# A convolution, attention and expert kernel: projection moved ahead of the next contraction, side work in other slots

## The chip, the cores and the metric

The kernel runs on one core of one Trainium2 chip. The metric is the device time of one execution in microseconds. The core has five engines that run side by side and wait for each other through semaphores: TensorE (PE), VectorE (DVE), ScalarE (ACT), GpSimd (POOL) and SyncE (SP), whose queue issues most DMAs. PE writes only to PSUM, which has eight banks of 128 x 512 fp32 numbers.

## The reference

Four images of 32 x 32 positions and 128 channels go through two layers, each added to its input.

1. A group norm, then a deformable convolution: eight groups of 32 channels, nine samples a position. Offsets, a scale and weights come from projections of the normalised image; each sample is a bilinear mix of four values; the eight groups' sums are projected by `out_w` and added to the image.
2. A layer norm and attention through 32 slices for each of eight heads, added; then a layer norm and a mixture of eight experts (128 to 512 to 128, exact GELU), of which each position uses its best two, added.

```python
x = x + conv(_gn(x), ...)
t = _to_tokens(x)
t = t + attn(_ln_t(t), ...)
t = t + ffn(_ln_t(t), ...)
```

## The kernel before

**Main loop.** The convolution is done as matrix products instead of gathers. There are 32 groups (`ig`, four images of eight), each of four batches (`beta`) of two half steps (`pair`), 256 half steps (`k`) in all. In a half step `distances` (L746) makes the distances of samples to grid rows and columns in banks 4 and 5; ACT turns the one into ramps (L1047, L1057), DVE (L1355, `take_y`) and POOL (L670, `ysb`) the other; `products` (L759) multiplies them, 64 small matmuls, into banks 0 and 1 (pair 0) or 2 and 3 (pair 1); DVE copies them out (L1365, `take`, into `asb`). The first three stages run three half steps ahead. After eight half steps `contract` (L774) contracts `asb` with the values into banks 0 to 3, ACT copies the result to `osp` (L1064, `spread_out`), `project` (L782) multiplies it by `out_w` into banks 2 and 3, and DVE adds it to the image (L1374, `conv_add`).

**Side work.** Each engine runs its own program in order. Between the half steps it calls `side` with a slot number. A group has nine slots, one for each half step and one more between the last products and the contraction; an image has 72. While image 0 is contracted, the slots hold the preparation of images 1 to 3 (`prepare`, 23 slots an image). While image b is contracted they hold image b-1's attention (23 pieces, `attend`, slots 2 to 30), the sorting of its tokens by expert (POOL, `sort_rows` L638, slots 29 to 36), the turning of the sorted rows (40 to 45) and its 23 expert tiles (46 to 69), and image b-2's picking and adding of rows (`pick_rows` L648, `add_rows` L1593, slots 1 to 17). A tile is `hidden` (L934, PE), `gelu` (L1132, ACT), `finish` (L947, PE) and `copy_rows` (L1583, DVE). All of this uses banks 6 and 7 alone, so each step of it waits until the step before has left them.

**Tail.** Behind the last contraction the attention and the experts of image 3 follow, with all eight banks and twelve buffers for expert weights instead of four; POOL picks image 2's rows first.

**Order.** It is written out by hand: the tables of slots at the top say on which engine which step is called when. At a group's start PE does the distances, the first side slot and the first products; then the distances, `project` of the group before, the second side slot; the second products wait for `conv_add`, since they write banks 2 and 3. DVE does `take_y`, the side slot, `take` in each half step, with `conv_add` ahead of the second.

## Time and profile before

| | us |
|---|---|
| median of three runs | 1490.27 (1489.19 to 1490.53) |
| the profiled execution | 1483.1, span 1481.2 |
| busy: PE, DVE, ACT, POOL | 1076.1, 907.2, 729.4, 695.7 |
| DMA | 80 GB/s in the mean |

An engine's busy time says how long it worked, not whether anyone waited for it. The span has four parts: what lies ahead of the first contraction (to 89.6 us), image 0's contraction with the preparation of the others (to 354.1), images 1 to 3 with the side work (to 1288.4), and the tail. Waits are put down to the instruction that released them. PE's busy time includes the modelled ends of pipelined matmuls.

### The profile page before, as it was taken

The page shows a single profiled execution, that of the slowest core. Times are in us where ns is not written, and L with a number is a line of the kernel's source. Part 1 is how long each engine was busy: PE and PEld are TensorE (multiplying, and loading weights), DVE is VectorE, ACT ScalarE, POOL GpSimd, SP SyncE. Part 2 cuts the span into 40 slices and gives each one's busy share as a digit, 9 for nine tenths or more (in the row PEclk, how much of TensorE's full clock was granted, in tenths as well). Part 3 has the DMA queues.
Part 4 walks back from the last instruction along what each step waited for, and adds up shares of the span by engine and source line. Part 5 has one row for each costly group of instructions (what it writes and reads, how often), then busy time and mean ns, then how long its engine had stood idle before and what let it go on. Part 6 is the DMA issues. An engine that isn't in the chain of part 4 may idle for free.

```text
span 1481.2 us, 62984 instructions
## 1 busy us (share of the span) xinstructions
PE 1076.1 (73%) x27983; PEld 879.2 (59%) x28236; DVE 907.2 (61%) x1619; ACT 729.4 (49%) x1403; POOL 695.7 (47%) x675
## 2 busy tenths in 40 slices
PE   3476766866886678986876789968866799765390
PEld 2365655645565568875565678856655688635290
DVE  7578775786756664458876564467666744454311
ACT  1454653545563456664643666655534566331060
POOL 6355544544432754457434744474427644510304
PEclk9598987999997899998987999999978999976595
DMA  6503222022000324631012325521103345200861
GB/s 143 143 27 92 67 47 96 27 54 99 24 26 15 105 76 125 177 101 35 26 40 84 90 64 160 148 68 31 35 22 99 83 139 151 73 9 1 254 185 55
DMA packets 166288, 121.96 MB, mean 82 GB/s; under 512 B 45641, under 2 KB 146050, under 8 KB 165506
## 3 DMA queue, kind: packets, MB, share of 16 engines
q1 hardware_dynamic: 161922, 109.53, 26.1%
q0 software_dynamic: 4096, 8.40, 1.8%
q8 instruction: 222, 3.64, 1.0%
q14 instruction: 48, 0.39, 0.1%
HBM read 89.38 MB, written 28.51 MB: 80 GB/s over the span
## 4 chain that ended last, share of the span: by engine, by line
PE 53%; DVE 25%; issue 11%; POOL 5%; ACT 3%; DMA 1%; another core or an unknown queue 1%; DVEq 0%; POOLq 0%; ACTq 0%
PE ps L774 13%; PE ps L759 12%; PE ps L934 6%; PE ps L947 6%; DVE asb L1365 5%; PE ps L746 4%; DVE yr L1355 4%; PE ps L782 3%; POOL ysb L670 2%; POOL picked L648 2%; DVE region L1577 1%; POOL sorted_rows L638 1%; DVE x_tok L1374 1%; PE ps L857 1%; PE ps L711 1%
## 5 line engine op out<-in xcount | busy, mean ns | idle before, releaser
L670 POOL TENSOR_TENSOR ysb<-yr,rw 128x512 f32<-128x512 f32 x512 | 547.1, 1093 | 567.3 <-DVE yr L1355 499.6
L1365 DVE COPY asb<-ps 128x1024 f32<-128x1024 f32 x256 | 312.0, 1219 | 126.1 <-PE ps L759 124.7
L759 PE MATMUL ps<-xsb,ysb 64*64 64x64 f32 x16384 | 324.2, 231 | 60.3 <-DVE x_tok L1374 38.3
L759 PEld LDWEIGHTS ps<-xsb,ysb 64*64 64x64 f32 x16384 | 287.0, 144 | 134.4 <-issue 111.4
L1057 ACT ACTIVATE xsb<-xr,pick 128x512 f32<-128x512 f32 x512 | 361.9, 764 | 4.4
L1355 DVE TENSOR_SCALAR yr<-ps 128x512 f32<-128x512 f32 x256 | 174.3, 681 | 218.1 <-PE ps L746 210.9
L774 PE MATMUL ps<-asb,vd 32*32 32x256 f32 x8192 | 204.2, 443 | 86.3 <-DVE asb L1365 68.3
L774 PEld LDWEIGHTS ps<-asb,vd 32*32 32x32 f32 x8192 | 146.1, 111 | 137.3 <-issue 109.8
L1047 ACT ACTIVATE xr<-ps 128x512 f32<-128x512 f32 x256 | 151.7, 593 | 137.4 <-remote 137.1
L746 PE MATMUL ps<-spread_b,lp 128*128 128x512 bf16 x259 | 105.5, 409 | 122.1 <-DVE yr L1355 51.1
L1064 ACT ACTIVATE osp<-ps 128x256 f32<-128x256 f32 x128 | 39.8, 405 | 277.3 <-PE ps L774 277.3
L1132 ACT ACTIVATE region<-ps,b_col 128x128 f32<-128x128 f32 x368 | 105.1, 370 | 88.5 <-PE ps L934 88.5
L638 POOL DMA_INDIRECT sorted_rows<-region,row_no x64 | 62.8, 982 | 116.2 <-DVE row_no L1545 100.5
L648 POOL DMA_INDIRECT picked<-expert_rows,row_no x64 | 61.7, 964 | 90.5 <-DMA expert_rows<-region 73.7
L746 PEld LDWEIGHTS ps<-spread_b,lp 128*128 128x128 bf16 x512 | 33.4, 98 | 117.9 <-DVE yr L1355 47.9
L934 PEld LDWEIGHTS ps<-region,ring 128*128 128x128 f32 x616 | 80.7, 195 | 9.5 <-issue 1.4
L934 PE MATMUL ps<-region,ring 128*128 128x128 f32 x616 | 83.6, 280 | 1.3 <-issue 1.3
L947 PE MATMUL ps<-ring,region 128*128 128x128 f32 x616 | 82.0, 276 | 0.0
L947 PEld LDWEIGHTS ps<-ring,region 128*128 128x128 f32 x616 | 75.7, 193 | 0.4
L1583 DVE COPY region<-ps 128x128 f32<-128x128 f32 x92 | 26.8, 291 | 74.8 <-PE ps L947 74.8
L782 PEld LDWEIGHTS ps<-outw,osp 128*128 128x128 f32 x512 | 62.1, 192 | 6.3 <-ACT osp L1064 1.8
L782 PE MATMUL ps<-outw,osp 128*128 128x128 f32 x512 | 62.4, 275 | 1.3 <-ACT osp L1064 1.3
(235 smaller groups left out, 1075.9 us busy)
## 6 DMA issues: line engine op xcount, KB each, us to landing
ring<-in_L_ffn_W SPq DMA_DIRECT2D x154, 256.0 KB, 3.1
vd<-group_values SPq DMA_DIRECT2D x128, 128.0 KB, 2.7
asb<-in_L_ffn_W SPq DMA_DIRECT2D x30, 256.0 KB, 4.3
lp<-position_parts SPq DMA_DIRECT2D x96, 64.0 KB, 2.4
position_parts<-region SPq DMA_DIRECT2D x3, 1536.0 KB, 6.0
group_values<-region SPq DMA_DIRECT2D x32, 128.0 KB, 3.5
weight_rows<-region SPq DMA_DIRECT2D x4, 1024.0 KB, 6.1
rw<-weight_rows SPq DMA_DIRECT2D x32, 128.0 KB
```

The source lines that it names most:

```text
L670: pl.tensor_tensor(ysb[:, n % 2, pair * CHUNK:(pair + 1) * CHUNK, u, :], yr[:, k % 3, :, :], rw[:, ig % 2, u, first:first + CHUNK].rearran ...
L746: pe.matmul(ps[:, bank, :], lp[:, ig % 2, beta, d, :], spread_b[:, half * CHUNK:(half + 1) * CHUNK, :].rearrange("p s q -> p (s q)"), star ...
L759: last = pe.matmul(o[:, :, NV * q:NV * q + NV], ysb[rows, n % 2, col, :, :].rearrange("p u y -> p (u y)"), xsb[rows, n % 2, col, :, :], st ...
L774: last = pe.matmul(ps[32 * jc:32 * jc + 32, j, 0:256], vd[rows, ig % 2, x, :], asb[rows, x, :, :, :].rearrange("p i n m -> p (i n m)"), st ...
L782: last = pe.matmul(pcol(2, t), osp[:, t, :], outw[:, ig % G, :], start=True, stop=True)
L934: last = pe.matmul(ps[:, hidden_bank(b, i), j * P:(j + 1) * P], ring_part(r, 0)[:, j * P:(j + 1) * P], xsT[:, i, :], start=True, stop=True)
L947: last = pe.matmul(ps[:, expert_bank(b, i), 0:C], hT[:, i % 2, j, :], ring_part(r, 1)[:, j * P:(j + 1) * P], start=(j == 0), stop=(j == HJ ...
L1047: act.activation(xr[:, half * CHUNK:(half + 1) * CHUNK, :].rearrange("p s q -> p (s q)"), ps[:, X_BANK, :], ACT.Relu, bias=1.0, scale=-1.0 ...
L1057: act.activation(xsb[:, n % 2, sets, :, v], xr[:, sets, :], ACT.Relu, bias=pick[:, v:v + 1], scale=-1.0).then_inc(s.x_ready, 1)
L1132: last = act.activation(hT[:, i % 2, j, :], ps[:, hidden_bank(b, i), j * P:(j + 1) * P], ACT.Gelu, bias=b1_col[:, i, j:j + 1])
L1355: dve.tensor_scalar(yr[:, k % 3, :, :].rearrange("p s q -> p (s q)"), ps[:, Y_BANK, :], 0.0, 1.0, ALU.max, ALU.min).then_inc(s.y_taken, 1)
L1365: dve.tensor_copy(asb[:, :, :, 2 * beta + pair, :].rearrange("p x i m -> p i x m"), ps[:, 2 * pair:2 * pair + 2, :].rearrange("p i (x m) - ...
```

## The change

- `project` of group g is called at the end of group g+1, in front of `contract`, and writes banks 6 and 7 (the last group: 2 and 3 as before). In an image's first group it is called in the second half step, for the image before. The second products wait for ACT's copies out of banks 2 and 3 instead of for `conv_add`. DVE calls `conv_add` behind the group's last `take`.
- Since banks 6 and 7 are the side work's too, PE waits ahead of `project` until the latest side step has been evacuated (`wait_for_banks`), and ahead of the next side slot until `conv_added`.
- A group has eight slots, an image 64. The tables are new. A slot serves image b-1 and, with its number raised by 64, image b-2 (`works`). The last expert tiles (slots 64, 66, 67, 68), the picking (72 to 79) and the adding (80 to 87) fall into the next image's first 24 slots. The tail goes through the same slots, now with image 2's last tiles, picking and adding in it.
- DVE's longer steps are cut into several with slots of their own: the reciprocal (two halves of 256 columns), statistics and normalisation, the choice of experts (`find_top`, `find_gates`), the columns (three parts), and in the preparation `find_places`, `split_places` and `edge_weights`.
- The attention's and the preparation's weights are turned in slot 5 instead of 69. `row_diff`, `parts_late`, `stage` and `rows_in` have other places in the shared region, and the waits that guard them have moved with them.
- The sort starts in slot 30, with the rows' numbers made in slot 29 (before: 29 and 27).

```diff
-ATTENTION = 23
-
-
-GROUP_SLOTS = 2 * BATCHES + 1
+
+
+GROUP_SLOTS = 2 * BATCHES
 SLOTS = G * GROUP_SLOTS
 
-PREP_SLOTS = 23
-PE_PREP = ((0, 0), (3, 2), (4, 3)) + tuple((7 + t, 4 + t) for t in range(NT)) + ((20, 13), (21, 14))
-ACT_PREP = ((0, 0), (4, 3), (15, 12), (20, 13), (21, 14))
-DVE_PREP = (((1, 1), (3, 2), (5, 3), (6, 15)) + tuple((7 + t, 4 + t) for t in range(NT))
-            + ((15, 16), (16, 12), (17, 19), (18, 17), (19, 18)))
-SP_PREP = ((14, 11), (19, 12), (21, 14))
-TURN_SLOT, BIAS_SLOT = PREP_SLOTS * (B - 1), PREP_SLOTS * (B - 1) + 2
-
-ATTENTION_SLOTS = (2, 3, 5, 6, 7, 8, 10, 11, 12, 13, 14, 15, 17, 18, 19, 20, 21, 22, 23, 24, 27, 29, 30)
-WEIGHT_SLOT = 28
-SORT_SLOT, SORT_SLOTS = 29, 8
-ROW_SLOT = 37
-TURN_ROWS_SLOT = 40
-TILE_SLOT = 46
-PICK_SLOT, PICK_SLOTS = 1, 8
-ADD_SLOT = 10
+PREP_SLOTS = 20
+COLUMN_SLOTS = (6, 7, 8, 9, 10, 11, 12, 12)
+PE_PREP = ((0, 0), (2, 2), (3, 3)) + tuple((COLUMN_SLOTS[t], 4 + t) for t in range(NT)) + ((19, 13), (20, 14))
+ACT_PREP = ((0, 0), (3, 3), (13, 12), (19, 13), (20, 14))
+DVE_PREP = (((1, 1), (2, 2), (4, 3), (5, 20), (5, 15)) + tuple((COLUMN_SLOTS[t], 4 + t) for t in range(NT))
+            + ((13, 16), (14, 12), (15, 21), (16, 22), (17, 19), (18, 23), (19, 17), (20, 18), (21, 24), (22, 25),
+               (23, 26)))
+SP_PREP = ((13, 11), (21, 14), (23, 12))
+TURN_SLOT = 5
+
+PE_STEPS = {5: ("turn_tn",), 6: ("xpT0",), 7: ("xpT1",), 8: ("temps",), 9: ("xp0",), 11: ("xp1",),
+            13: ("logits0",), 14: ("logits1",), 15: ("logits2",), 16: ("logits3",), 17: ("turn_e0",),
+            18: ("turn_e1",), 19: ("sums",), 20: ("M",), 21: ("out",), 25: ("turn_xt",), 26: ("router",),
+            29: ("ranks",), 30: ("turn_gate",), 31: ("b2",)}
+ACT_STEPS = {3: ("std",), 5: ("tnT",), 6: ("xpT0",), 7: ("xpT1",), 13: ("logits0",), 14: ("logits1",),
+             15: ("logits2", "exp0"), 16: ("logits3",), 17: ("exp1", "e0"), 18: ("e1",), 20: ("M",), 23: ("std1",),
+             25: ("xt",), 26: ("std2",), 27: ("exp",), 30: ("gateT",)}
+DVE_STEPS = {2: ("stats",), 4: ("normalise",), 5: ("bout",), 8: ("temps",), 9: ("recip0",), 10: ("xp0",),
+             11: ("recip1",), 12: ("xp1",), 13: ("logits0",), 14: ("logits1", "max0"), 15: ("logits2",),
+             16: ("logits3", "max1"), 18: ("norms",), 19: ("bdE",), 21: ("add",), 22: ("stats1",),
+             24: ("normalise1",), 25: ("stats2",), 26: ("top",), 27: ("normalise2",), 28: ("gates",), 29: ("rows",),
+             30: ("columns0",), 31: ("b2",), 32: ("columns1",), 33: ("columns2",)}
+WEIGHT_SLOT = 30
+SORT_SLOT, SORT_SLOTS = 30, 8
+ROW_SLOT = 38
+TURN_ROWS_SLOTS = (40, 40, 41, 41, 42, 42)
+TILE_SLOTS = tuple(range(44, 65)) + (66, 67, 68)
+PICK_SLOT, PICK_SLOTS = 72, 8
+ADD_SLOT = 80
+LAST_SLOT = ADD_SLOT + PICK_SLOTS
+assert len(TILE_SLOTS) == ROWS + 1 and len(TURN_ROWS_SLOTS) == TURNS
...
+def works(b, slot):
+
+    return [(image, at) for image, at in ((b - 2, slot + SLOTS), (b - 1, slot)) if image >= 0]
+
+
+def last_of(table, slot):
+
+    return [step for when, step in table if when < slot][-1:]
...
+        def project_bank(ig):
+
+            return 6 if ig < IMAGES_GROUPS - 1 else 2
...
-                    last = pe.matmul(pcol(2, t), osp[:, t, :], outw[:, ig % G, :], start=True, stop=True)
+                    last = pe.matmul(pcol(project_bank(ig), t), osp[:, t, :], outw[:, ig % G, :], start=True, stop=True)
...
+            def wait_for_prepared(b, step):
+
+                if step == 0:
+                    pe.wait_ge(s.x_copied, b + 1)
+                elif step == 2:
+                    pe.wait_ge(s.spread, b + 1)
+                elif step == 3:
+                    pe.wait_ge(s.group_std, b + 1)
+                elif 4 <= step < 12:
+                    pe.wait_ge(s.columns_biased, NT * b + step - 3)
+                else:
+                    pe.wait_ge(s.rows_copied, 2 * b + step - 12)
+
+            def wait_for_step(b, step):
+
+                if step == "turn_tn":
+                    pe.wait_ge(s.tnT_copied, b + 1)
+                elif step in ("xpT0", "xpT1"):
+                    pe.wait_ge(s.xpT_copied, 2 * b + int(step[-1]) + 1)
...
+                else:
+                    pe.wait_ge(s.b2_added, b + 1)
+
+            def wait_for_banks(b, slot):
+
+                if b == 0:
+                    for image_no in range(1, B):
+                        for step in last_of(PE_PREP, slot - PREP_SLOTS * (image_no - 1)):
+                            wait_for_prepared(image_no, step)
+                    if slot > TURN_SLOT:
+                        pe.wait_ge(s.turned_copied, 2)
+                        pe.wait_ge(s.ln_cols_copied, 4)
+                    return
+                for image_no, at in works(b, slot):
+                    for step in last_of([(when, step) for when in PE_STEPS for step in PE_STEPS[when]], at):
+                        wait_for_step(image_no, step)
+                    for q in last_of([(TURN_ROWS_SLOTS[q], q) for q in range(TURNS)], at):
+                        pe.wait_ge(s.tiles_scaled, TURNS * image_no + q + 1)
+                    for i in last_of([(TILE_SLOTS[i], i) for i in range(ROWS + 1)], at):
+                        pe.wait_ge(s.hidden_ready, ROWS * image_no + min(i + 1, ROWS))
+                        pe.wait_ge(s.expert_copied, ROWS * image_no + i)
...
-                    if ig and beta == 0 and pair:
+                    g, at = ig % G, 2 * beta + pair
+                    slot = g * GROUP_SLOTS + at
+                    if g == 0 and ig and at == 1:
+                        wait_for_banks(ig // G, slot)
                         project(ig - 1)
-                    side(ig // G, ig % G * GROUP_SLOTS + 2 * beta + pair)
+                    if at == 0 and ig >= 2:
+                        pe.wait_ge(s.conv_added, ig - 1)
+                    elif g == 0 and ig and at == 2:
+                        pe.wait_ge(s.conv_added, ig)
+                    side(ig // G, slot)
                     pe.wait_ge(s.x_ready, NV * (k + 1))
                     pe.wait_ge(s.y_ready, NU * (k + 1))
                     if beta:
                         pe.wait_ge(s.a_taken, k - 1)
-                    elif ig and pair == 0:
-                        pe.wait_ge(s.out_copied, 4 * (ig - 1) + 2)
                     elif ig:
-                        pe.wait_ge(s.conv_added, ig)
+                        pe.wait_ge(s.out_copied, 4 * (ig - 1) + 2 * pair + 2)
                     products(n, pair)
                 if beta == BATCHES - 1:
-                    side(ig // G, (ig % G + 1) * GROUP_SLOTS - 1)
+                    if ig % G:
+                        wait_for_banks(ig // G, (ig % G + 1) * GROUP_SLOTS)
+                        project(ig - 1)
                     contract(ig)
             project(IMAGES_GROUPS - 1)
-            for k in range(ATTENTION):
-                attend(B - 1, k)
-            for q in range(TURNS):
-                turn_rows(B - 1, q)
-            for i in range(ROWS + 1):
-                tile(B - 1, i)
+            pe.wait_ge(s.conv_added, IMAGES_GROUPS - 1)
+            for slot in range(LAST_SLOT + 1):
+                side(B, slot)
...
+                elif step == "recip0":
+                    dve.reciprocal(rtemp[:, 0:256], temp_sb[:, 0:256])
+                elif step == "recip1":
+                    dve.reciprocal(rtemp[:, 256:512], temp_sb[:, 256:512]).then_inc(s.rtemp_ready, 1)
...
-                    if beta == 0 and pair == 1 and ig:
+                    if beta == 0 and pair == 1 and ig and ig % G == 0:
                         conv_add(ig - 1)
                     side(ig // G, ig % G * GROUP_SLOTS + 2 * beta + pair)
                     take(n, pair)
-                if beta == BATCHES - 1:
-                    side(ig // G, (ig % G + 1) * GROUP_SLOTS - 1)
+                if beta == BATCHES - 1 and ig % G:
+                    conv_add(ig - 1)
             conv_add(IMAGES_GROUPS - 1)
-            for k in range(ATTENTION):
-                attend(B - 1, k)
-                if k == 4:
-                    for m in range(TOP * NT):
-                        add_rows(B - 2, m)
-            for q in range(TURNS):
-                scale_rows(B - 1, q)
-            for i in range(ROWS):
-                copy_rows(B - 1, i)
-            for m in range(TOP * NT):
-                add_rows(B - 1, m)
+            for slot in range(LAST_SLOT + 1):
+                side(B, slot)
```

## Rows read from the trace of the kernel before

**Rows 1.** The page: busy us, share of the span, instructions of an engine.
```profile
PE 1076.1 (73%) x27983; PEld 879.2 (59%) x28236; DVE 907.2 (61%) x1619; ACT 729.4 (49%) x1403; POOL 695.7 (47%) x675
```

**Rows 2.** Busy time by stage: stretch, its length, then each engine's busy time.
```profile
core 0: us, PE busy (x) PEld busy (x) DVE busy (x) ACT busy (x) POOL busy (x), PEclk, DMA share, GB/s
...
89.60:354.10 264.50, 188.67 (x5962) 149.23 (x6024) 194.09 (x246) 133.66 (x220) 134.92 (x112) 0.88 0.25 67
...
663.00:976.20 313.20, 249.01 (x6951) 206.35 (x6998) 199.75 (x353) 174.18 (x342) 163.07 (x161) 0.92 0.28 81
...
1288.40:1481.20 192.80, 101.95 (x619) 84.89 (x613) 65.79 (x234) 47.83 (x122) 40.37 (x42) 0.71 0.33 99
```

**Rows 3.** One boundary in order of time: start, length, engine and line, idle time before.
```profile
1145.62 3.02 PE L774 MATMUL ps<-asb,vd 32*32 32x256 f32 x110
...
1148.67 1.25 ACT L1064 ACTIVATE osp<-ps 128x256 f32<-128x256 f32 x4 [6.52 <-PE ps L774]
...
1150.99 0.38 PE L746 MATMUL ps<-spread_b,lp 128*128 128x512 bf16 x1 [0.16 <-issue]
...
1151.20 1.95 PE L782 MATMUL ps<-outw,osp 128*128 128x128 f32 x16
...
1153.19 1.22 DVE L1374 TENSOR_TENSOR x_tok<-x_tok,ps 128x1024 f32<-128x1024 f32 x1 [0.50 <-PE ps L782]
...
1154.56 1.16 PE L759 MATMUL ps<-xsb,ysb 64*64 64x64 f32 x64 [1.41 <-DVE x_tok L1374]
...
1155.77 1.22 DVE L1365 COPY asb<-ps 128x1024 f32<-128x1024 f32 x1 [1.37 <-PE ps L759]
...
1172.62 6.67 PE L774 MATMUL ps<-asb,vd 32*32 32x256 f32 x256 [3.00 <-DVE asb L1365]
```

**Rows 4.** Waits over the span: us in total, times, longest.
```profile
PE ps L774 <- DVE asb L1365: 68.3, 25, 8.0
...
PE ps L759 <- DVE x_tok L1374: 38.3, 17, 9.0
```

**Rows 5.** Busy time: image 0's seven stretches, all 32 contractions, three of image 2's.
```profile
sum 208.60, PE 139.21 PEld 111.65 DVE 183.88 ACT 133.66 POOL 131.13; mean PE 19.89 PEld 15.95 DVE 26.27 ACT 19.09 POOL 18.73
...
sum 207.60, PE 188.97 PEld 145.34 DVE 29.21 ACT 2.37 POOL 38.33; mean PE 5.91 PEld 4.54 DVE 0.91 ACT 0.07 POOL 1.20
...
745.00:787.70 42.70, 29.89 (x656) 26.26 (x645) 35.32 (x111) 21.48 (x37) 15.56 (x16) 0.84 0.12 34
868.20:898.10 29.90, 28.12 (x678) 26.00 (x667) 18.59 (x26) 25.50 (x60) 16.43 (x16) 1.00 0.40 117
904.70:936.20 31.50, 30.23 (x713) 28.37 (x688) 18.22 (x25) 25.21 (x63) 16.43 (x16) 1.00 0.55 165
```

**Rows 6.** DVE by line, image 2's stage and the tail: busy us, mean ns.
```profile
L1404 DVE TENSOR_TENSOR x_tok<-x_tok,boutb_b 128x1024 f32<-128x1024 f32 x1 | 4.3, 4312 | 0.0
...
L1404 DVE TENSOR_TENSOR x_tok<-x_tok,boutb_b 128x1024 f32<-128x1024 f32 x1 | 1.2, 1226 | 0.0
```

**Rows 7.** POOL in order of time, in image 1's stage.
```profile
484.61 1.16 POOL L638 DMA_INDIRECT sorted_rows<-region,row_no  x1 [10.84 <-DVE row_no L1545]
...
503.01 2.06 POOL L670 TENSOR_TENSOR ysb<-yr,rw 128x512 f32<-128x512 f32 x2
...
507.52 2.06 POOL L670 TENSOR_TENSOR ysb<-yr,rw 128x512 f32<-128x512 f32 x2
```

**Rows 8.** ACT by line, image 2's stage.
```profile
L1132 ACT ACTIVATE region<-ps,b_col 128x128 f32<-128x128 f32 x92 | 26.3, 371 | 13.9 <-PE ps L934 13.9
```

**Rows 9.** The tail's beginning in order of time.
```profile
1296.08 0.30 ACT L1072 ACTIVATE f_sd<-f_mv,eps_col 128x8 f32<-128x8 f32 x1 [4.67 <-DVE f_mv L1388]
...
1298.95 1.97 PE L795 MATMUL ps<-ident,region 128*128 128x128 f32 x8 [6.74 <-DVE region L1399]
```

488 lines of the change are left out of this document (254 added, 234 removed).

## The prediction

> **What bounds the kernel now.** I read the page's shares of busy time first: no engine is busy all the time, PE 73%, DVE 61%, POOL 47% [rows 1]. So the limit changes from stage to stage, and the next view is busy time by stage [rows 2]. While image 0 is contracted DVE has 194.1 of 264.5 us; while image 2 is contracted PE has 249.0 of 313.2 us and DVE 199.8; behind the last contraction (192.8 us) PE is about half busy and a chain of dependent steps sets the time. The 32 groups between 89.6 and 1288.4 hold 1199 us, so what happens once per group matters most.
>
> Then one boundary between two groups, in order of time [rows 3]. The contraction (L774) ends at 1148.64. ScalarE copies the result out (1.25 us), PE projects it (L782, 1151.20, 1.95 us) into banks 2 and 3, DVE adds it to the image (L1374, 1153.19, 1.22 us), and only then may the products of the second half step, which need banks 2 and 3, start (1154.56). DVE takes them at 1155.77. The reader is to see a chain PE, ACT, PE, DVE, PE in which nothing of the main loop advances. At the other end the contraction waits 3.00 us for DVE's last take [rows 3]. Over the run PE waits 68.3 us (25 times) for that take and 38.3 us (17 times) for the add [rows 4].
>
> Last, the stretches between contractions [rows 5]. They are of two kinds. With attention work woven in (745.0 to 787.7) DVE is busy 35.3 of 42.7 us; with expert tiles woven in (904.7 to 936.2) PE is busy 30.2 of 31.5, and in the stretch before it 28.1 of 29.9. Image 0's seven stretches are DVE's too: 183.9 of 208.6 us.
>
> **The change part by part.**
>
> *Projection moved.* The projection of group g goes from the start of group g+1 to its end, in front of the contraction, into banks 6 and 7. The second products then wait only for the four copies out (over at 1149.92), for the distances, and for PE itself, so they start where the projection started: 1154.56 - 1151.20 = 3.36 us earlier [rows 3]. For DVE the gain is the same: its take follows 3.36 us earlier, and the add (1.22 us) now runs beside the next contraction, where it has nothing else to do. The seven groups behind image 0's first, and the five attention or near-empty groups of each later image (15), are of the kind where this is felt. But at an image's first boundary (3 of these 22) the projection stays in front of the second products and the add in front of DVE's take; only PE's wait for the add goes, 1 us each. That makes 19 x 3.36 + 3 = 67 us. In the nine stretches with expert tiles (three an image) PE is the bound, the side tile already lies in the wait for the add, and no more than PE's idle 1.3 to 1.8 us is to be had [rows 5]: I take 1 us each, 9 us.
>
> *Its price at the back.* Eight matmul pairs, 1.95 us, now stand between the last products and the contraction. The mean wait there is 68.3 / 25 = 2.7 us [rows 4], so mostly they are hidden; where DVE is prompt the wait is the take's 1.22 us and two hand-overs, 1.4 us, and the projection sticks out by 0.6. The bound is 0 to 28 x 0.6 = 17 us; I take 5, since most waits are longer. In front of it PE also waits until the last side step's result has left banks 6 and 7. DVE and ACT do that before their own part of the last half step, so the bound is 0 to 1 us a group; behind this wait stand the projection and the contraction, and for them ACT's copy out. I take 0, with 28 us as the far end. The wait for the add ahead of the next side work is covered by the contraction's 6.5 us.
>
> *The ninth slot goes.* Each group had nine slots of side work for eight half steps, and DVE did the ninth beside the contraction. In all 32 contractions DVE is busy 29.2 us [rows 5]. That cover is lost: the same work now stands in the stretches. Some 24 us of it is in stretches that DVE bounds, and costs its full length; bounds 10 and 29.
>
> *Smaller steps.* The reciprocal, the place finding, the splitting, the edge weights, the normalisations and the column sums are cut up and spread. The durations are conserved (the reciprocal's two halves cost one more start, under 0.2 us), so nothing is gained where DVE is the bound. What can be gained is that a take and a distance step come between the pieces, so that PE and POOL run dry less: this is part of the 68.3 us. Bounds 0 and 30 us; I take 12, below the middle, because the heaviest attention stretch already has DVE busy for 83% of it, and with the picks and adds of the image before moved behind, two stretches (slots 16 to 31) carry that load. One operation shows how uneven the cost is: the add of the output bias (L1404, two SBUF inputs) took 4.31 us in image 2 and 1.23 us in the tail [rows 6].
>
> The Trainium skill ("SBUF — State Buffer", the section on the shared port pair) says that a VectorE operation with two SBUF inputs and a GpSimd operation exclude each other for a whole instruction. The 4.31 us against 1.23 agrees with it, though those rows do not show the cause. By that rule a denser POOL stream would lengthen such pieces by up to about 3 us in each of three images, 9 us in all; my sum leaves this out, and it lies within the range.
>
> *Last tiles moved, sorting closer to its input.* Tiles 20 to 22 go to the next image's first slots. In images 1 and 2 the work is only moved. For image 2 it lands in the tail. There a woven tile is serial: the hidden matmuls, four GELU pieces of 0.37 us [rows 8] and the output matmuls, about 3 us a tile. ACT does the last tile's GELU before the square root of the attention's statistics, which before was ready at 1296.08, so that the first transposition at 1298.95 [rows 9] comes some 5.5 us later. The reciprocal's second half stands behind one add of 1.2 us, and the normalisation in front of the gates costs 0.5: the tail is 7 us longer, bounds 2 and 15. The 16 pickings of image 2 start later too, but POOL is free there, and their adds come only beside the attention's logits.
>
> *POOL.* The sort's first slot is 30, one behind the slot of the rows (29); it was two. POOL runs up to three half steps ahead and waited 10.84 us for the row numbers [rows 7]; then a half step with two sorts costs it 507.52 - 503.01 = 4.51 us instead of 2.06. I count 0 for it, and the rest as a rival. New slot tables for SP move its issues with the work they serve; no queue has a transfer that was late, so 0 again.
>
> Sum: -67 - 9 + 5 + 24 - 12 + 7 = -52 us. The profiled execution has a span of 1481.2 us (1483.1 with what lies around it); it would become 1429. The median of the three runs is 1490.27, 7.2 us above the profiled one, and by the same difference becomes **1438 us**.
>
> **The rivals.**
>
> *Every boundary pays (1403 us, chance 0.20).* If the smaller steps hide what the ninth slot hid, and the expert stretches gain too, then 28 x 3.36 = 94 us fall away and the tail's 7 come back: 1490 - 87. For it: PE idles 68.3 us ahead of contractions for a DVE that is late. Against it: PE's 30.2 of 31.5 us.
>
> *DVE keeps the time (1474 us, chance 0.19).* DVE's own work in the loop is conserved. If attention stretches stay bound by it and the steps wait for each other one slot apart, only the add's 1.22 us is saved, in 19 groups (23 us), and 7 us go to the tail: -16. For it: 183.9 of 208.6 in image 0. Against it: DVE really idles at each boundary.
>
> *POOL becomes the bound behind the sort (1510 us, chance 0.07), slower than before.* With one slot less between rows and sort, POOL loses its lead in every image: eight half steps at 4.51 where the others need about 3.3 (29.9 us for nine slots; 10 us), and three half steps of lead to fill again at 4.51 (14 us), 24 an image, 72 in three. It decides from 52 / 3 = 17 us an image on. For it: the wait of 10.84 us is there already. Against it: in the whole of image 2 POOL is busy 163 of 313 us [rows 2], and the contraction lets it catch up.
>
> *The change doesn't do what it says (1488 us, chance 0.04).* If the wait for banks 6 and 7 regularly ends behind DVE's last take, the projection lies open again, at the group's end instead of its start. Then only the add's overlap remains and the lost slot eats it.
>
> **How the numbers follow.** The forecast of 1438 has 0.50. The range must leave out no more than 0.2: it goes from just under the first rival's time, 1400, to a little over the second's, 1480, which leaves out the slower rival, the ineffective change and a little at the fast end. 0.2% of 1490 is 3 us, about what a measurement here can tell from no change. Faster: 0.50 + 0.20 + 0.19 and little of the fourth rival, 0.89; the same 0.04; slower 0.07.
>
> **What would show it.** In the profile after: the second products about 3 us behind the contraction's end instead of 5.92; the add at L1374's place inside the contraction; no PE wait for it. PE's wait ahead of the contraction shrinks from 68 us to under 30. Expert stretches shorten by a tile's 2 us, because they hold eight instead of nine, and no more. DVE's busy time inside contractions is about 28 x 1.22 us = 34. The tail is 197 to 203 us. If the stretches with attention work don't get shorter, the DVE rival holds; if PE waits for ysb behind each sort, the POOL rival. I am wrong if the added waits let the engines run in step, so that each half step becomes the sum of two engines.

## The result, and the profile after

| | us |
|---|---|
| before, same chip, median of 4 | 1489.73 (1487.03 to 1490.53) |
| after, median of 4 | 1465.09 (1461.05 to 1468.37) |
| ratio | 0.9847, 95% interval 0.9828 to 0.9866 |
| the profiled execution of after | 1466.5, span 1464.1 |

The change gains 24.6 us (20 to 26 by the interval), where 52 were forecast. By the profiled spans it is 1481.2 to 1464.1, or 17 us, because the profiled execution of before (1483.1 us) was shorter than any of the four. The figures below are of spans, so they account for 17 us and not for the other 7.

One view for each kernel, by the same cuts, gives the sum. The stretches between contractions went from 208.6 to 217.9 us in image 0, from 256.5 to 245.4 in image 1, from 264.9 to 253.9 in image 2 and from 261.3 to 255.3 in image 3; the 31 contractions behind the first from 201.6 to 192.1; the tail from 192.9 to 205.4. These figures run from the start of a contraction's first weight load to the end of its last one (L774 before, L787 after); the matmuls themselves end some 0.5 us later. So images 1 to 3 gain 28 us, the contractions 9.5, and image 0 and the tail give back 22. Of the 28 us, only 4.4 come from the nine stretches with expert tiles (270.5 to 266.1), and 23.7 from the others.

Busy time by stage of after (the columns of [rows 2]): image 0, image 2, the tail; then one heavy attention stretch and one expert stretch (as [rows 5]); and the sum over all 32 contractions.

```profile
89.00:356.90 267.90, 203.90 (x6014) 148.33 (x6016) 195.38 (x241) 133.41 (x214) 146.26 (x112) 0.90 0.25 66
651.60:955.20 303.60, 264.94 (x7004) 205.94 (x6997) 198.59 (x354) 174.71 (x342) 164.53 (x160) 0.93 0.30 84
1258.60:1464.10 205.50, 115.32 (x670) 91.77 (x670) 66.29 (x239) 51.35 (x134) 45.98 (x48) 0.69 0.32 97
...
464.50:506.90 42.40, 30.97 (x622) 24.57 (x611) 35.03 (x103) 19.98 (x33) 19.76 (x20) 0.78 0.28 81
578.60:608.30 29.70, 29.70 (x695) 26.55 (x680) 17.00 (x24) 24.39 (x60) 16.45 (x16) 1.00 0.60 170
...
sum 197.18, PE 177.46 PEld 131.34 DVE 32.95 ACT 2.89 POOL 27.38; mean PE 5.55 PEld 4.10 DVE 1.03 ACT 0.09 POOL 0.86
```

DVE's work is conserved (image 2: 198.6 us, [rows 2] 199.8). The expert stretch holds PE for its whole 29.7 us. Each image still has one heavy attention stretch, now its fourth instead of its third, and it is as long as before's (42.4 against 42.7, DVE 35.0 against 35.3). DVE is busy 33 us in the contractions, where 34 were forecast for the adds alone.

The boundary that answers to [rows 3], in order of time. The contraction ends at 1118.84 (1118.21 + 0.63).

```profile
1118.21 0.63 PE L787 MATMUL ps<-asb,vd 32*32 32x256 f32 x6 [0.54 <-issue]
...
1119.70 1.16 PE L772 MATMUL ps<-xsb,ysb 64*64 64x64 f32 x64 [0.33 <-ACT osp L1145]
1120.02 3.42 DVE L1661 TENSOR_TENSOR region<-region,b_turned 128x184 f32<-128x184 f32 x4
1120.19 2.52 POOL L686 TENSOR_TENSOR ysb<-yr,rw 128x512 f32<-128x512 f32 x2 [0.87 <-DVE yr L1438]
...
1121.33 1.03 PE L772 MATMUL ps<-xsb,ysb 64*64 64x64 f32 x53
...
1123.47 1.23 DVE L1448 COPY asb<-ps 128x1024 f32<-128x1024 f32 x1
...
1125.21 0.91 DVE L1666 TENSOR_REDUCE b_col<-region 128x92 f32<-128x736 f32 x1
...
1126.03 1.22 DVE L1448 COPY asb<-ps 128x1024 f32<-128x1024 f32 x1
...
1143.03 3.29 PE L795 MATMUL ps<-outw,osp 128*128 128x128 f32 x16
1143.14 1.23 DVE L1448 COPY asb<-ps 128x1024 f32<-128x1024 f32 x1 [2.85 <-PE ps L772]
...
1146.35 1.22 DVE L1457 TENSOR_TENSOR x_tok<-x_tok,ps 128x1024 f32<-128x1024 f32 x1 [1.99 <-PE ps L795]
```

The second products start 2.5 us behind the contraction's end (before 5.9), as forecast. But DVE takes them 7.2 us behind it, and before it was 7.1 [rows 3]: the 3.4 us are gone, because DVE's piece of side work (L1661, 3.4 us) stands ahead of the first take, and another (L1666, 0.9 us) ahead of the second. Over all 31 boundaries, measured from the last weight load, the second products start 5.21 us behind the end (before 8.06) and the second take 7.98 (before 9.64): the products gain 2.85 us and the take 1.66. DVE's side work ahead of the second take sums to 3.52 us in the mean, where it was 2.35: the new tables put more of it there. Below, "the second take" is always this mean.

PE's waits over the span (us, times, longest), against [rows 4]:

```profile
PE ps L759 <- DVE yr L1438: 47.9, 29, 3.7
...
PE ps L787 <- DVE asb L1448: 23.9, 10, 4.4
PE ps L787 <- issue: 19.3, 29, 1.8
PE ps L735 <- DVE region L1421: 17.4, 4, 9.2
```

The wait for the add (38.3 us) has left the list and the one ahead of the contraction went from 68.3 to 23.9. The latter is partly a change of label, since the projection, about 2 us each time, now fills that place: from the last products to the contraction it is 3.06 us in the mean, before 3.04.

The tail's beginning (as [rows 9]) and its logits:

```profile
1270.70 0.29 DVE L1680 COPY region<-ps 128x128 f32<-128x128 f32 x1 [1.31 <-PE ps L1023]
...
1273.46 1.97 PE L871 MATMUL ps<-ident,region 128*128 128x128 f32 x8 [2.81 <-DVE region L1480]
...
1290.17 1.91 PE L915 MATMUL ps<-region,ws_bd 128*128 128x512 f32 x2 [2.21 <-DVE region L1497]
1292.01 2.07 PE L916 MATMUL ps<-region,head_pick 32*128 32x512 f32 x2
```

The first transposition stands 14.8 us behind the last contraction's end (1258.6), before 10.6 (1298.95 [rows 9], less 1288.4): the three tiles cost 4.2 us. (In f1, e3b and g3 below, where no tile runs in the tail, it stands 10.6 to 11.0 us behind again.) The eight pairs of logits run at half pace, which is taken up below.

### The profile page after: what moved, and what is told of

Its sections match the earlier page's. It is cut to its first block, busy times and chain, and to the rows that moved or that the text cites. A ratio compares the mean times of both kernels' runs of the same rounds, so it can differ in the third digit from the quotient of the medians.

```text
span 1464.1 us, 63368 instructions
## 1 busy us (share of the span) xinstructions
PE 1143.3 (78%) x28236; PEld 873.2 (60%) x28236; DVE 908.5 (62%) x1623; ACT 732.3 (50%) x1403; POOL 712.6 (49%) x675
## 4 chain that ended last, share of the span: by engine, by line
PE 39%; DVE 17%; issue 6%; POOL 3%; ACT 2%; DMA 1%; POOLq 0%; DVEq 0%; ACTq 0%
PE ps L787 9%; PE ps L772 7%; PE ps L1010 6%; PE ps L1023 5%; PE ps L759 3%; PE ps L795 3%; DVE asb L1448 3%; DVE yr L1438 2%; DVE region L1674 2%; DVE x_tok L1690 1%; POOL sorted_rows L655 1%; PE ps L916 1%; PE ps L915 1%; POOL picked L665 1%; PE ps L969 1%
## 5 line engine op out<-in xcount | busy, mean ns | idle before, releaser
L686 POOL TENSOR_TENSOR ysb<-yr,rw 128x512 f32<-128x512 f32 x512 | 563.8, 1125 | 520.0 <-DVE yr L1438 466.9
L1438 DVE TENSOR_SCALAR yr<-ps 128x512 f32<-128x512 f32 x256 | 174.4, 681 | 207.2 <-PE ps L759 201.6
L759 PE MATMUL ps<-spread_b,lp 128*128 128x512 bf16 x512 | 176.5, 411 | 68.6 <-DVE yr L1438 47.9
L787 PE MATMUL ps<-asb,vd 32*32 32x256 f32 x8192 | 192.5, 407 | 43.3 <-DVE asb L1448 23.9
L787 PEld LDWEIGHTS ps<-asb,vd 32*32 32x32 f32 x8192 | 131.4, 106 | 96.3 <-issue 66.5
L795 PE MATMUL ps<-outw,osp 128*128 128x128 f32 x512 | 72.6, 300 | 13.5 <-DVE x_tok L1579 7.4
L795 PEld LDWEIGHTS ps<-outw,osp 128*128 128x128 f32 x512 | 66.9, 210 | 14.9 <-DVE x_tok L1579 7.8
```

Source lines behind the costliest of these rows:

```text
L686: pl.tensor_tensor(ysb[:, n % 2, pair * CHUNK:(pair + 1) * CHUNK, u, :], yr[:, k % 3, :, :], rw[:, ig % 2, u, first:first + CHUNK].rearran ...
L759: pe.matmul(ps[:, bank, :], lp[:, ig % 2, beta, d, :], spread_b[:, half * CHUNK:(half + 1) * CHUNK, :].rearrange("p s q -> p (s q)"), star ...
L787: last = pe.matmul(ps[32 * jc:32 * jc + 32, j, 0:256], vd[rows, ig % 2, x, :], asb[rows, x, :, :, :].rearrange("p i n m -> p (i n m)"), st ...
L795: last = pe.matmul(pcol(project_bank(ig), t), osp[:, t, :], outw[:, ig % G, :], start=True, stop=True)
L1438: dve.tensor_scalar(yr[:, k % 3, :, :].rearrange("p s q -> p (s q)"), ps[:, Y_BANK, :], 0.0, 1.0, ALU.max, ALU.min).then_inc(s.y_taken, 1)
```

## The experiments

The kernel before took between 1539 and 1546 us in most of the groups of runs below, and 1485 to 1490 in two of them (the first, and that of g1 to g4). A ratio is always against the kernel before of its own group; "long groups" and "short groups" are meant by this. The chip does not explain the two kinds: the group of c0 and that of g1 ran on the same one, and the kernel before took 1541 us in the one and 1485 in the other.

**Theory.** A boundary gives less than 3.36 us, because DVE's side work in the first slots fills the time; the rest of the miss lies in image 0 and the tail. **Rivals:** the lost ninth slot costs more than forecast; the smaller steps bring nothing; the projection in front of the contraction costs what it saves.

### One part undone or done alone

e1b and f3 are one and the same kernel, the changed one with the projection back behind the next group's first products:

```
-            return 6 if ig < IMAGES_GROUPS - 1 else 2
+            return 2
...
-                        wait_for_banks(ig // G, (ig % G + 1) * GROUP_SLOTS)
-                        project(ig - 1)
```

> The changed kernel with the projection back at the group's start in banks 2 and 3 and the add ahead of the second take; tables, small steps and eight slots stay. Theory A (the move is the gain, but only what side work did not already fill counts): in the profile after, DVE's second take starts 7.98 us behind a contraction's end in the mean, against 9.64 before, 1.66 us instead of the 3.36 forecast; undone at 28 boundaries that is 46 us, so about 1510 us, slower than the kernel before as well. Theory B (DVE keeps the time, the gain of 25 us came from the smaller steps): 1470 to 1480.

> The changed kernel with the projection put back behind the next group's first products (banks 2 and 3), all else as changed; this time on the same chip as the changed kernel, so that the two ratios can be divided. If the projection's new place is worth what its first look against another chip's run said: 0.022 of the time, 33 us, a little over 1 us for each of 31 boundaries. By the forecast's 3.36 us for each of 28: 94 us too much in this order, since the smaller slot would add its own. By the 1.66 us that the second take of a group moved: some 50 us at most. Rival (the first look's difference was the chip's): under 0.010, 15 us. The idle time of TensorE in front of second products goes back to about 70 us put down to VectorE.

Measured: e1b 0.9928 (0.9892 to 0.9964); f3 0.9928 (0.9902 to 0.9955), and f0, the changed kernel in f3's group, 0.971. 1529.2 - 1493.4 = 36 us, 1.2 for each of 31 boundaries. The second take is at 9.73 us in f3 and at 7.98 in f0 (1.75 x 31 = 54 us), while the way from the last products to the contraction is 2.21 against 2.89 (21 us back): 33 us, which fits. The projection's place is worth half of the forecast's 71, in a long group; no run undoes it in a short one. As a ratio, e1b falls where theory B put it (1470 to 1480 us are 0.987 to 0.993), but only because the whole change is worth more in long groups; the difference of 36 us is nearer to theory A's 46 than to B's 5 to 15. f3's expectation of 33 us holds, but not its wait: PE waits 21.7 us for the add ahead of the second products, not 70, and 71.7 for the last take.

e2b is the kernel before with the projection moved, and nothing else:

```
+                    if ig % G:
+                        wait_for_banks(ig // G, (ig % G + 1) * GROUP_SLOTS)
+                        project(ig - 1)
                     contract(ig)
```

> The kernel before with the projection moved in front of the contraction into banks 6 and 7 and nothing else: nine slots, the old tables, long steps, tail as before. Theory A: the move is worth about 46 us and none of the costs of the other parts is there (image 0's stretches 9 us longer, tail 12.6 us longer), so about 1445 us, faster than the full change. Theory B (DVE keeps the time): 1480. If the projection behind the ninth slot only lengthens the way to the contraction: 1490.

Measured: 0.9977 (0.994 to 1.0013), nothing that can be told from no change. This is the third of its expectations. The gain of a boundary is there: against c0, the kernel before in another long group, the second products start 3.3 us sooner and the second take 2.0 (7.80 against 9.79). But the contraction starts 4.54 us behind the last products (c0: 2.88), 51 of the 62 us that the takes gain over 31 boundaries. One group's end in e2b:

```profile
1193.99 1.21 DVE L1434 COPY asb<-ps 128x1024 f32<-128x1024 f32 x1
1195.12 1.35 DVE L1646 TENSOR_SCALAR region<-ps,scale_col,shift_col 128x128 f32<-128x128 f32 x4
1196.73 3.75 PE L785 MATMUL ps<-outw,osp 128*128 128x128 f32 x16 [4.37 <-DVE region L1646]
1200.41 1.11 PE L777 MATMUL ps<-asb,vd 32*32 32x256 f32 x32
```

DVE does the ninth slot's piece behind its last take, the projection waits for that piece because it needs the banks, and only then comes the contraction. What the ninth slot hid beside the contraction now stands in front of it. The forecast had named this wait and priced it at nothing.

e3b is the changed kernel with nine slots a group; g3 is the same with the gathers held (below). Both have tables to match: the preparation takes 23 slots an image again, and all expert tiles lie inside their image's slots.

```
-GROUP_SLOTS = 2 * BATCHES
+GROUP_SLOTS = 2 * BATCHES + 1
...
+                    side(ig // G, (ig % G + 1) * GROUP_SLOTS - 1)
                     if ig % G:
                         wait_for_banks(ig // G, (ig % G + 1) * GROUP_SLOTS)
```

> The changed kernel with nine slots a group again (72 an image), the preparation spread over 23 slots an image, all expert tiles inside the image's slots, small steps and moved projection kept. Theory A: the eight-slot tables are what gives the gain back, in image 0 (17 to 20 us) and in the tail (4 us of woven tiles), so 1435 to 1445 us. Theory C (small steps cost hand-overs, the number of slots doesn't matter): within 5 us of the changed kernel, 1460 to 1470.

Measured: 0.9898 (0.9824 to 0.9973), against 0.970 for the changed kernel in such groups: nine slots with their tables are 30 us slower (give or take 11), not 24 faster, and neither theory had that. Image 0 alone liked them (201.2 us of stretches, against 216 to 218). The way to the contraction is 4.78 us.

e5b has eight slots, but DVE's long steps joined again:

```
-DVE_STEPS = {2: ("stats",), 4: ("normalise",), 5: ("bout",), 8: ("temps",), 9: ("recip0",), 10: ("xp0",),
+DVE_STEPS = {2: ("stats",), 4: ("normalise",), 5: ("bout",), 8: ("temps", "recip0", "recip1"), 10: ("xp0",),
...
-             30: ("columns0",), 31: ("b2",), 32: ("columns1",), 33: ("columns2",)}
+             24: ("normalise1", "stats2"), 27: ("normalise2", "top", "gates"), 29: ("rows", "columns0", "columns1", "columns2"),
```

> The changed kernel with DVE's steps put together again in one slot each (reciprocal, add with statistics, both normalisations with their statistics, choice of experts, rows with columns, place finding, edges, splitting), in the eight-slot tables. My forecast gave the small steps 12 us: then 1477. Theory C (each small step is one more hand-over one slot apart): 1455 to 1465.

Measured: 0.9873 (0.9835 to 0.991), 25 us slower than the changed kernel in such groups, twice the forecast's 12; theory C is out. The view of PE's waits says where:

```profile
PE ps L759 <- DVE yr L1438: 73.0, 31, 5.4
...
PE ps L787 <- DVE asb L1448: 19.6, 9, 4.7
```

PE waits 73 us for the distances' copy, 25 more than after (and than f0, 48.0), in about as many waits, the longest 5.4 instead of 3.7. The wait ahead of the contraction didn't grow. The smaller steps gain, but by a wait the forecast had not looked at.

### The same two kernels elsewhere, and the last contraction

> The kernel before, unchanged, as a control on the chip of this group: ratio 1.00 within the noise. Its trace is wanted beside those of the others, since this chip may run all of them slower. Every theory expects 1.00.

> The changed kernel, unchanged, as a control beside the variants: 0.985 of the kernel before, if the gain is not a matter of the chip. If PE's waits for its own instructions, long on one chip, hide gains, the ratio comes nearer to 1: 0.99.

Measured in a long group: before again 0.9976 (0.995 to 1.0002), the change 0.9703 (0.9662 to 0.9743). So the change is worth 3% there and 1.5% in the short group; neither 0.985 nor 0.99, the two values that c1's expectation named. The spans differ by 39 us (1532.0, 1492.8), and 19 of them are in one place, the last contraction: 26.2 us against 7.3. In the short group's profile of before it took 7.4. POOL and then PE in c0, each in order of time:

```profile
1307.12 1.00 POOL L648 DMA_INDIRECT picked<-expert_rows,row_no  x1 [7.20 <-DMA expert_rows<-region]
1308.43 0.97 POOL L648 DMA_INDIRECT picked<-expert_rows,row_no  x1 [0.30 <-issue]
...
1325.95 0.95 POOL L648 DMA_INDIRECT picked<-expert_rows,row_no  x1 [0.30 <-issue]
...
1307.56 7.57 PE L774 MATMUL ps<-asb,vd 32*32 32x256 f32 x85 [1.42 <-DVE asb L1365]
1315.48 1.06 PE L774 MATMUL ps<-asb,vd 32*32 32x256 f32 x4 [0.35 <-issue]
1316.90 1.09 PE L774 MATMUL ps<-asb,vd 32*32 32x256 f32 x5 [0.36 <-issue]
...
1322.59 1.08 PE L774 MATMUL ps<-asb,vd 32*32 32x256 f32 x3 [1.06 <-issue]
1324.01 0.58 PE L774 MATMUL ps<-asb,vd 32*32 32x256 f32 x1 [0.35 <-issue]
...
1329.62 4.60 PE L774 MATMUL ps<-asb,vd 32*32 32x256 f32 x145 [0.39 <-issue]
```

All 16 gathers of image 2's expert rows, one each 1.25 us, lie beside it; from 1315 us on PE gets a few matmuls every 1.4 us and otherwise waits for nothing that the profile shows, until it is back at full pace 2.7 us behind the last gather's end. f2 tests this with the kernel before:

```
                     if b:
                         pl.wait_ge(s.rows_added, TOP * NT * b)
+                    if b == B - 2:
+                        pl.wait_ge(s.out_summed, IMAGES_GROUPS)
```

> The changed kernel once more, beside the three others of this group. On the chip of its first run it took 0.985 of the time of the kernel before, on a second chip 0.970, where the kernel before ran some 50 us longer. Theory A (the ratio differs because the kernel before has a stretch of its own that is long on some chips: its last contraction took 26.2 us there and 7.4 us here, with 16 gathers of expert rows beside it): the ratio goes with the length of that contraction, near 0.97 where it is over 20 us and near 0.985 where it is under 8. Theory B (all stretches of the nine-slot order are more sensitive to the chip): the ratio goes with the time of the kernel before, whatever that contraction takes. The tail's eight logit products take 16 us (2.07 us a pair) again.

> The kernel before with one wait more: GpSimd begins the 16 gathers of image 2's expert rows behind the last contraction instead of as soon as the rows are stored. Theory A (TensorE's instructions come late while the gathers run: in the last contraction its records have gaps of 0.4 to 1.1 us put down to issue, one about every 1.4 us, and the gathers follow each other at 1.25 us): where the kernel before has its last contraction at 26 us this one has it at 6 to 8, and the time is 15 to 20 us shorter, ratio 0.987 to 0.990; the gathers may take some us in the tail instead. Rival B (the contraction is late for another reason, such as its place in the program): it stays at 26 us and the ratio is 1.000 within 0.002. On a chip where the contraction takes 7 us in the kernel before, both give 0.998 to 1.002.

Measured: f0 0.971 (0.9688 to 0.9733), which doesn't separate its two theories; f2 0.9951 (0.9933 to 0.997). f2's last contraction takes 7.4 us, as theory A has it, but its time is only some 7 us shorter, not 15 to 20. Its window of busy time in c0, and then in f2 (columns as in [rows 2]):

```profile
1307.50:1333.70 26.20, 20.23 (x252) 7.27 (x256) 0.00 (x0) 0.00 (x0) 14.83 (x16) 0.54 0.15 41
```

```profile
1317.90:1325.30 7.40, 5.60 (x253) 3.78 (x256) 0.00 (x0) 0.00 (x0) 0.00 (x0) 1.00 0.02 4
```

So the gathers stretch the contraction: shown. By what way is open. Theory A's guess, instructions that come late, finds no support in the transfers of the instruction queue: in c0 the trace has none between 1310.5 and 1330.5, and the next one begins when PE has been back at full pace for a microsecond, so none of them ended the slow stretch. The Trainium skill ("Runtime: NRT & Kernel Launch", section "Instruction fetch mechanics") says that fetching the instructions is mostly hidden behind the work; that goes with what the queue shows, and leaves the cause of the slow stretch unnamed. The tail gave back 11 us of the 19 in f2 (209.5 against 198.3), since DVE then waited 11.1 us for the gathered rows ahead of the reciprocal, and the logits came late and ran at half clock.

The changed kernel gets the 19 us as a by-product. Image 2's last tiles run in the tail, so its rows are stored later and the gathers start behind the contraction. It keeps nearly all of the 19 us, which f2 did not: its tail is longer than before's by 13.7 us in the long group of c0 and c1, and by 12.5 in the short one. f1 gives the counterproof, as it lets the tiles end within the image:

```
-TILE_SLOTS = tuple(range(44, 65)) + (66, 67, 68)
+TILE_SLOTS = (43, 44, 45, 45, 46, 47, 47, 48, 49, 49) + tuple(range(50, 64))
```

> The changed kernel with three edits of its tables: the edge weights of the next image's grid are made one slot sooner (measured alone: image 0's stretches 216.2 to 214.6 us, the whole 0.9692 against 0.9703), both halves of the attention's reciprocal stand ahead of the two token projections (alone: the tail 212.0 to 208.2), and the last three expert tiles run inside the image's own slots, two in a slot, instead of in the tail and in the next but one image's first slots. If the gains add: 1.6 + 4 us, and in the tail the three tiles no longer stand ahead of the first turning (the changed kernel's stands 14.5 us behind the last contraction, before 10.6): another 4, together 9 to 10 us or a ratio 0.006 under the changed kernel's. Rival: four slots with two tiles each hold TensorE 1.3 us longer a tile in images 2 and 3 and give the 4 us back, 0.002 to 0.004 under it. Second rival: the tail's other engines take over (the attention's exponentials) and nothing is gained behind 4 us.

Measured: 0.989 (0.985 to 0.993), 27 us slower than f0 (20 by the profiled spans) instead of 9 faster. The tail is 198.9 us (f0 211.6), but slots with two tiles lengthen image 1 by 8.6 us, and

```profile
1286.80:1314.20 27.40, 19.71 (x252) 6.84 (x256) 1.22 (x1) 0.00 (x0) 15.17 (x16) 0.65 0.15 40
```

the 16 gathers lie beside the last contraction again, and it takes 27.4 us. Neither of the expectation's rivals had this.

> The changed kernel with nine slots a group (0.990 of the kernel before, against 0.970 with eight), and image 2's gathers held until the last contraction is over. If the gathers explain part of the nine slots' cost: the last contraction 17.2 us there becomes 6 to 8 here, about 10 us, of which the kernel before with the same wait gave half back in the tail: ratio 0.984 to 0.987, so that the ninth slot by itself costs 20 us, near the 24 less 29 of the forecast's bounds. If the gathers have nothing to do with it, 0.990 stays and the contraction stays at 17 us.

Measured, in a short group: 0.9937 (0.9912 to 0.9961), the last contraction 5.5 us. Against the 0.9847 of the change in the other short group that is 13 us for nine slots by themselves. The other 17 of e3b's 30 are in sight: its last contraction, with seven of the gathers beside it, took 17.2 us, 11.7 more than g3's, and PE stood idle for 5.1 us right ahead of it, beside the gathers before those, put down to issue. The expectation's 0.984 to 0.987 was meant for a long group and can't be held against this one.

### What holds the take, and what was to be had back

g2 puts DVE's take of the second slot ahead of that slot's side work:

```
-                    side(ig // G, ig % G * GROUP_SLOTS + 2 * beta + pair)
-                    take(n, pair)
+                    if ig and beta == 0 and pair == 1:
+                        take(n, pair)
+                    side(ig // G, ig % G * GROUP_SLOTS + 2 * beta + pair)
+                    if not (ig and beta == 0 and pair == 1):
+                        take(n, pair)
```

> The changed kernel with one reordering on VectorE: in the second slot of each group the copy of the group's second products stands ahead of that slot's side work instead of behind it. Theory (the boundary gave 1.7 us instead of 3.4 because VectorE's side work of the first two slots, not the image add, is what the copy waits behind): the second take starts under 7.4 us behind a contraction's end instead of 7.98, TensorE's wait for VectorE's copies (25 us in all) falls, and the kernel gains 5 to 20 us, up to 0.7 us a boundary for 31 boundaries. Rival: the take waits for TensorE's products, which themselves come no sooner, and the side work is merely late instead, whose waits on TensorE grow: no change, within 3 us, or slower by up to 10.

Measured: 0.9996 (0.9973 to 1.0019), some 22 us slower than the changed kernel's 0.9847 (14 by the profiled spans). The second take does come sooner, at 7.04 us instead of 7.98, so the side work was what it stood behind: this 0.94 and the change's 1.66 make 2.60 of the 2.85 us that the products gained. But from there to the group's last take it is 22.71 us instead of 21.31, and PE waits 65.2 us for the distances' copy instead of 47.9. The work is only pushed along: the theory of what holds the take is right, and its hope of a gain is wrong. The rival holds, at more than the loss of up to 10 us that it named.

e4 makes image 0's edge weights one slot sooner; e6 puts both halves of the reciprocal ahead of the token projections:

```
-            + ((13, 16), (14, 12), (15, 21), (16, 22), (17, 19), (18, 23), (19, 17), (20, 18), (21, 24), (22, 25),
+            + ((13, 16), (14, 12), (15, 21), (15, 22), (16, 19), (17, 23), (19, 17), (20, 18), (21, 24), (22, 25),
```

```
-PE_STEPS = {5: ("turn_tn",), 6: ("xpT0",), 7: ("xpT1",), 8: ("temps",), 9: ("xp0",), 11: ("xp1",),
+PE_STEPS = {5: ("turn_tn",), 6: ("xpT0",), 7: ("xpT1",), 8: ("temps",), 11: ("xp0",), 12: ("xp1",),
...
-DVE_STEPS = {2: ("stats",), 4: ("normalise",), 5: ("bout",), 8: ("temps",), 9: ("recip0",), 10: ("xp0",),
-             11: ("recip1",), 12: ("xp1",), 13: ("logits0",), 14: ("logits1", "max0"), 15: ("logits2",),
+DVE_STEPS = {2: ("stats",), 4: ("normalise",), 5: ("bout",), 8: ("temps",), 9: ("recip0",), 10: ("recip1",),
+             11: ("xp0",), 12: ("xp1",), 13: ("logits0",), 14: ("logits1", "max0"), 15: ("logits2",),
```

> The changed kernel, image 0's preparation alone altered: the edge weights one slot earlier (slots 16 and 17 instead of 17 and 18), the clipping of places in slot 15, so that PE's turning in slot 19 stands two slots behind its input. In the changed kernel PE waited 8.1 us for it (three times) and 24 us for preparation steps in all, against 4 before. Theory A (steps one slot apart stall PE, and with it DVE): 5 to 8 us below the changed kernel. Theory D (DVE's own work bounds image 0, PE's waits there cost nothing): the same as the changed kernel.

> The changed kernel with both halves of the reciprocal in slots 9 and 10 and the two additions in 11 and 12. In the changed kernel's tail PE stood idle 2.21 us for the second half, and the logits behind it ran at a granted clock of 0.51 for 16.1 us, where before they had 1.00 and 8.6 us. Theory A (the order cost the clock): the tail 8 to 9 us shorter. Rival: the clock falls elsewhere or whatever the order, tail the same within 2 us.

Measured in c1's group (0.9703): e4 0.9692 (0.9651 to 0.9733), e6 0.9681 (0.9629 to 0.9733). In the whole time neither can be told from the changed kernel. In image 0 of after PE waits 8.1 us for the turning of those weights:

```profile
L735 PE MATMUL ps<-ident,region 128*128 128x128 f32 x48 | 9.4, 360 | 8.1 <-DVE region L1421 8.1
```

In e4 this wait is gone, but image 0's stretches shrink by 1.6 us only; PE waits 17.9 us instead of 13.0 for the distances' copy and 11.8 instead of 7.9 ahead of the contraction. A wait for DVE that goes comes back as another one while DVE sets the pace: theory D, not A. In e6 the logits run at full clock again, 8.5 us instead of 16.1, but the tail is only 3.8 us shorter, 208.2 instead of 212.0, which is neither of its expectations. Part of the gain comes back behind the logits, where PE waits 6.0 us instead of 2.3 for ACT's exponentials.

g1 and h1 have both edits, g4 has g2's as well, and h0 is the changed kernel beside h1.

> The changed kernel with two of the three repairs of f1: edge weights one slot sooner, reciprocals together; the last expert tiles stay where the change put them. If what f1 lost came from the tiles alone: last contraction 6 to 8 us, image 1's stretches near 246, the tail near 208, the whole 4 to 6 us under the changed kernel's (on a chip where that one takes 0.970 to 0.971 of the kernel before: 0.967). Rival: the two together give no more than either alone, 0.970.

> The changed kernel with the two repairs of g1 and the reordering of g2. If both gain, by their sum: about 0.960 to 0.965 of the kernel before on a chip where the changed kernel takes 0.970. If g2's side work turns into waits of TensorE: g1's time and some us more.

> The changed kernel as the partner of the next one. If the group is one where the kernel before takes 1485 to 1490 us: 0.985; where it takes 1539 to 1543: 0.970.

> Edge weights one slot sooner and reciprocals together, beside the changed kernel. If the tail's gain of 4 to 6 us is real and image 0's 1 to 2: 0.003 to 0.005 under its partner's ratio. Rival: noise of places in the program, within 0.002 of it.

Measured: g1 1459.3 us, 0.9823 (0.9785 to 0.9861), g4 0.9918 (0.989 to 0.9947), both in the short group, so that g2's reordering costs some 15 us here too; h0 1498.6 us, 0.9676 (0.9636 to 0.9715), and h1 1488.4 us, 0.9617 (0.958 to 0.9655). Side by side the two edits gain 10 us (7.3 by the profiled spans), 0.006 of the kernel before, a little more than the 0.003 to 0.005 expected. 6.5 are in the tail (208.1, 214.6), and image 0 has none of it (218.0, 218.1). This is the fastest version of the study. The logits in g1:

```profile
1293.59 1.13 PE L915 MATMUL ps<-region,ws_bd 128*128 128x512 f32 x2 [1.08 <-DVE region L1497]
1294.65 1.12 PE L916 MATMUL ps<-region,head_pick 32*128 32x512 f32 x2
1295.70 1.12 PE L915 MATMUL ps<-region,ws_bd 128*128 128x512 f32 x2
```

## Where the prediction held, and where it failed

**Direction and range held; of the forecast gain of 52 us less than half came, 24.6.** Most signs that the prediction named came: at the boundary of [rows 3] the second products 2.5 us behind the contraction, no wait for the add, 23.9 us of wait ahead of the contraction, 33 us of DVE inside the contractions. What failed is the gain that was worked out from them. Its own steps in turn:

- *Projection moved, -67 and -9, its price +5: the step that failed.* "For DVE the gain is the same: its take follows 3.36 us earlier." The products do start sooner, by 2.85 us in the mean. But DVE was not idle for all of that time: the side work of the group's first two slots stands ahead of the takes in its order and had partly run within the old wait, and the new tables put 1.2 us more of it there. The take gains 1.66 us. I read the single boundary of [rows 3], where DVE happened to have no side work in either slot, and multiplied it by 19. The undoing measures 36 us in a long group, where 71 were forecast. In the expert stretches 9 us were forecast: one of them goes from 31.5 to 29.7, but all nine together give 4.4.
- *The projection's own length, 1.95 us.* In its new place the 32 projections take 72.6 us together instead of 62.4: most take 2.02 to 2.05 us, and six 2.3 to 3.8, at a lower granted clock. The price of +5 had no term for these 10 us.
- *The wait for banks 6 and 7, priced at 0.* Right with eight slots (3.06 us from the last products to the contraction, before 3.04). With nine the way is 1.7 us longer a group and eats most of the gain (e2b); some 0.5 of the 1.7 is the projection at the lower clock.
- *The ninth slot, +24.* Wrong in sign. Going from nine slots and their tables to eight, while the projection stands at the group's end, gains 13 us in a short group and 30 in a long one. The parts don't add up, since the ninth slot and the new projection stand one behind the other. In long groups the projection alone (e2b) gives 3 us, the tables and steps alone (f3) 11, and both together 45. Of these three only e2b still has the gathers beside the last contraction. A sum of terms can't show this; the terms that share a place have to be laid out in order of time.
- *Smaller steps, -12.* They are worth some 25 us (e5b), within the bounds of 0 to 30. They act on the wait for the distances' copy, not on the one ahead of the contraction.
- *Image 0.* Forecast to gain at each of its boundaries; its stretches are 9.3 us longer, and with its contractions it stands at +4.3. Of the DVE rival's two reasons, that steps one slot apart wait for each other is worth 1.6 us by e4. That DVE's own work sets the pace goes with it better, as [rows 5] had said (183.9 of 208.6 us; now 187.5 of 217.9). With the preparation over 23 slots an image instead of 20 the stretches take 201.2 and 201.6 us (e3b, g3), so what costs here is the denser table or the missing ninth slot; no run separates these two. In images 1 to 3 the rival's sign, attention stretches that don't get shorter, didn't come.
- *The tail, +7.* It is +12.5. The tiles were forecast at 5.5 and cost 4.2. The reciprocal's 1.2 us became 2.21 and then some 7.5, because TensorE's clock fell, though e6 got only 3.8 of this back. The windows over the logits, of after and then of before, show it (the third column from the end is the clock):

```profile
1290.00:1306.10 16.10, 15.93 (x17) 3.91 (x18) 5.16 (x9) 4.58 (x6) 3.68 (x4) 0.51 0.08 21
```

```profile
1314.70:1323.30 8.60, 8.50 (x16) 2.36 (x16) 5.62 (x8) 3.46 (x5) 0.00 (x0) 1.00 0.00 0
```

- *POOL, 0.* Right, the rival didn't come. The bias add that took 4.3 us [rows 6] takes 1.2 in all images of after. POOL's products take 1125 ns in the mean instead of 1093, and one pair beside DVE's L1661 took 2.52 us instead of 2.05. The Trainium skill ("SBUF — State Buffer", section "Who interferes with whom") lets whichever of the two comes second wait; the trace agrees with it. Before, in image 2, the bias add began at 693.02, 0.8 us behind the start of a POOL product, and took 4.31 us beside four of them in a row. In after's main loop it begins 0.2 us ahead of one, in all three images, and keeps its 1.21 us, and the POOL product takes 1.91 us, where the ones beside the slow add took 1.04. The 9 us that the prediction worked out by this rule were not seen.

**What the forecast had no term for.** In the groups where the kernel before takes 1540 us, the move of the last tiles takes the gathers away from the last contraction, 19 us. This brings the change near the forecast's ratio there (0.970 against 1438 / 1490 = 0.965). That is luck: the cause isn't one that the forecast held.

**Open.** Why all kernels take some 30 to 50 us longer in most groups than in two of them, by what way the gathers slow TensorE, and why six of them beside before's last contraction left it at 7.4 us in a short group, where seven (e3b) made it 17.2 and sixteen 26.2 in long ones. What the projection's place is worth in a short group, the kind of the forecast's own result, wasn't measured. Holding the gathers until a later place of the tail wasn't tried.

## What to carry to other kernels

Before multiplying the gain of one boundary, check for each kind of boundary what stands ahead of the freed instruction in its own engine's order: an earlier producer is worth only what the consumer spent waiting. When two moved pieces end up in the same place, lay them out in order of time instead of adding their prices; here the two parts were worth 3 and 11 us alone and 45 together. And look at what a later or an earlier step does to the start of DMAs: here the gathers' start was worth 19 us where it fell beside the last contraction.
